# A graph network of three layers on one core: weights that have only a bias between them multiplied once, the node's own rows added behind W1, and the last round's kept sums added by VectorE

## The chip, the cores and the metric

One NeuronCore of a Trainium2 chip. The metric is the device time of one execution in microseconds (us). The kernel before takes 2256.65 us (median of 3 runs, 2256.49 to 2256.9).

## What is computed

12,500 nodes with 64 values each, 400,000 edges (`src`, `dst`), three layers. In every layer each node adds up the messages of its neighbours, adds its own row, and goes through a small network of two weights:

```python
h = relu(layernorm(x))
for l in range(3):
    mlp = lambda z: relu(z @ W1[l] + b1[l]) @ W2[l] + b2[l]
    agg = segment_sum(mlp(h[dst]), src, 12500)
    h = mlp(h + agg)
return x + h @ Wf + bf
```

Between the ReLU of one layer and the next ReLU stand only `@ W2[l] + b2[l]` and `@ W1[l+1] + b1[l+1]`, and behind the last ReLU `@ W2[2] + b2[2]` and `@ Wf + bf`.

## The kernel before

The sum over the edges is done as dense matmuls. A first part sorts nothing but counts: from windows of the edge list it builds a matrix of edge counts (12,544 by 12,544, two counts of 4 bits to a byte) in `counts_dram`. Then `agg` is messages times counts. The messages are held as two halves of 16 bits (`parts`, an upper half made by ScalarE and a lower half made by VectorE, both scaled by a power of two from the largest message, so that `scal[:, l, 6:7]` undoes the scale). A tile of counts is 128 by 896 columns and comes by DMA, 7 tiles (784 KB) to a transfer; VectorE unpacks it into low and high nibbles (`spread`).

The columns are cut into SB = 7 stretches of 4 banks of 448 columns. A bank is one PSUM bank and collects its sum over 98 tiles of 128 rows.

**Layer 0** runs while the counts are built. The rows come in 7 rounds of 14 tiles; a unit is one round for one stretch, so there are 49 units, numbered 0 to 48. 41 of them (FUSED) run inside the build, the other 8 behind it. Since PSUM can't hold 28 banks, each unit's sum is copied out (`keep_sums`, ScalarE, into `acc_low`, which lies in `msg`, and `acc_high`), and the next round's unit begins by adding it again with a matmul by the identity (`add_kept`, L1331). Units 42 to 48 are the last round, one for each stretch, and their sums are read by VectorE.

**Layers 1 and 2** have 7 stretches each, of CH = 14 chunks; a chunk is 7 tiles for 4 banks, 28 matmuls of 448 columns (L1438). The first and the last chunk of a stretch go bank by bank.

Behind each stretch comes its epilogue, spread over the next stretch's chunks (or, in layer 0, over the next unit's blocks, by the table MLP_AT). In the kernel before:

- `read_sums` (VectorE, L881 and L882): for each bank two instructions of 64 partitions each, one that only scales the sum, one that scales it and adds the node's own rows from `hT`; into `zP`.
- u0, u1 (TensorE, L1392): `W1` times `zP`, in PSUM banks 4 and 5; ScalarE adds b1 and applies ReLU into `U` (L1200).
- h (TensorE, L1400): `W2` times `U`; ScalarE adds b2 into `hN` (L1209), and GpSimd copies it to `hT` as the own rows of the next layer (`save_h`, L619).
- v (TensorE, L1400 too): the next layer's `W1` times `hN`; ScalarE adds its b1, ReLU, into `V` (L1213).
- m0, m1 (TensorE, L1416): `V` times the next `W2`, which gives the next messages; VectorE adds b2 and finds the largest (`finish`, L894 and L897). In the last layer there is no v, and m multiplies `hN` by `Wf` and VectorE adds bf and x (L904, L909).

All matmuls of the epilogue are of 32-bit numbers, and each stands in the trace as two matmul records.

Engines work through their instructions in program order, so the place of a step in an engine's list decides what waits behind it. Three places matter here. In the last round VectorE does, for unit i, `read_sums` of unit i-1, `unpack_tail` of its second chunk, `finish` of unit i-2, `unpack_tail` of the next unit's first chunk. Between layer 0 and layer 1 it does `find_peak` (L811), unpacks one chunk, then `make_scale` (L821 to L825), which waits for GpSimd's maximum over the partitions (`share_peak`, L613), then four `lower_parts` (L832), then `read_sums` of unit 48, for which TensorE's first chunk of layer 1 waits. And behind the first stretch of layer 1 it runs `judge` (L805, L806), two long reductions that check the counts.

The build is 49 steps of HG = 4 groups (k = 0 to 195): VectorE makes one-hot tiles (L752), GpSimd weighs them (L627), TensorE multiplies them (L1307), ScalarE keeps the product (`keep_batch`, L1132), VectorE transposes it (L760). In groups 0 to 25 ScalarE also makes layer 0's first rows (L1092), `keep_h0` (L1122) and the ReLU of W1 times them (L1183).

## Time and profile before

| | |
|---|---|
| median of 3 runs | 2256.65 us |
| the profiled execution | 2256.61 us, of which the span of the trace is 2254.9 us |
| TensorE busy (PE, matmuls) | 2096.7 us, 93% |
| VectorE busy (DVE) | 1512.7 us, 67% |
| ScalarE busy (ACT) | 663.7 us, 29% |
| GpSimd busy (POOL) | 643.7 us, 29% |
| mean granted TensorE clock | 0.976 of full speed |
| DMA engines | 153 GB/s on average |

The profile has one row for each group of instructions by line of the kernel, a chain of waits followed back from the last instruction, and a timeline. PE is TensorE's matmul part and PEld its weight loads, which overlap. The span falls into setup (to about 75 us), build with layer 0's units 0 to 40 (to about 950 us), the units 41 to 48 (to 1104 us), layer 1 (to 1675 us) and layer 2 (to the end).

### The profile page before, as it was taken

Reading aid. Unit: us, or ns where it says so; the run is one execution under the profiler, and the core shown is the slowest. Engines: PE = TensorE matmul, PEld = TensorE weight load, DVE = VectorE, ACT = ScalarE, POOL = GpSimd, SP = SyncE. Lnnn points to the kernel's source line nnn. Section 1 sums busy time; section 2 is a strip of 40 time slices with the busy share of each in tenths; the row PEclk is TensorE's granted clock in tenths of the full one; section 3 lists DMA queues with packets and bytes.
Section 4 is the critical chain, followed back from the end, with each engine's and each line's share of the span. In section 5 each row is a group of like instructions: output and inputs, shape, how many; then the busy total and the mean of one; then the engine's idle time right before and its main releaser. Section 6 shows DMA issues by size and latency. Waiting matters only on the chain.

```text
span 2254.9 us, 39446 instructions
## 1 busy us (share of the span) xinstructions
PE 2096.7 (93%) x15866; PEld 1153.6 (51%) x15866; DVE 1512.7 (67%) x1683; ACT 663.7 (29%) x1632; POOL 643.7 (29%) x287
## 2 busy tenths in 40 slices
PE   3566779999999999999997999999999999999998
PEld 3444445555555555545553555555555555555554
DVE  7899999999999999846645434444463443444344
ACT  4885655555555555411200000000010000000000
POOL 3666667777767776500000000000000000000000
PEclk8796999999999999999998999999999999999999
DMA  7256666666666666642343435444444554555552
GB/s 194 71 139 180 178 181 189 182 188 196 190 188 193 185 187 176 186 125 72 122 127 110 146 111 160 151 128 145 143 132 134 157 165 126 169 159 159 145 157 68
DMA packets 332824, 344.46 MB, mean 153 GB/s; under 512 B 21562, under 2 KB 303992, under 8 KB 332184
## 3 DMA queue, kind: packets, MB, share of 16 engines
q1 hardware_dynamic: 327516, 335.59, 50.6%
q0 software_dynamic: 2352, 6.43, 1.1%
q8 instruction: 94, 1.54, 0.3%
q10 hardware_dynamic: 2816, 0.53, 0.2%
q14 instruction: 46, 0.38, 0.0%
HBM read 252.58 MB, written 89.89 MB: 152 GB/s over the span
## 4 chain that ended last, share of the span: by engine, by line
PE 80%; DVE 13%; issue 4%; DMA 2%; SPq 0%; ACT 0%; POOL 0%; DVEq 0%; POOLq 0%
PE ps L1438 46%; PE ps L1336 18%; DVE arena L752 6%; PE ps L1331 5%; PE ps L1307 5%; PE ps L1400 2%; DVE arena L760 2%; PE ps L1392 2%; PE ps L1416 1%; DMA arena<-counts_dram 1%; DVE arena L791 1%; DVE arena L799 1%; DVE arena L725 1%; SPq L439 0%; DVE msg L778 0%
## 5 line engine op out<-in xcount | busy, mean ns | idle before, releaser
L1438 PE MATMUL ps<-arena,parts 128*128 128x448 fp8e4 x5488 | 1054.0, 353 | 11.9 <-DVE arena L882 11.9
L1438 PEld LDWEIGHTS ps<-arena,parts 128*128 128x128 f16 x5488 | 535.1, 98 | 531.4 <-issue 44.7
L627 POOL TENSOR_TENSOR arena<-arena,weight_now 128x416 int32<-128x416 int32 x196 | 540.8, 2759 | 274.0 <-DVE arena L752 273.3
L866 DVE TENSOR_SCALAR arena<-arena 128x3136 uint16<-128x3136 uint16 x196 | 191.5, 977 | 624.5 <-PE ps L1438 617.9
L1336 PE MATMUL ps<-arena,parts 128*128 128x448 fp8e4 x2744 | 554.9, 353 | 1.5 <-DVE parts L832 1.5
L752 DVE TENSOR_TENSOR arena<-row_iota,key_now 128x4096 f16<-128x4096 f16 x196 | 446.3, 2277 | 0.0
L1336 PEld LDWEIGHTS ps<-arena,parts 128*128 128x128 f16 x2744 | 267.1, 98 | 296.9 <-issue 83.1
L1132 ACT ACTIVATE arena<-ps 128x800 uint16<-128x800 f32 x392 | 332.3, 874 | 73.2 <-PE ps L1307 64.1
L1200 ACT ACTIVATE arena<-ps,b1s 128x448 f32<-128x448 f32 x42 | 26.6, 634 | 943.5 <-PE ps L1392 943.5
L1307 PE MATMUL ps<-arena 128*128 128x53 fp8e4 x6272 | 204.3, 189 | 79.8 <-DVE arena L752 41.2
L1307 PEld LDWEIGHTS ps<-arena 128*128 128x128 f16 x6272 | 187.7, 98 | 151.4 <-DVE arena L752 95.5
L619 POOL COPY hT<-arena 128x896 f32 (+1 forms) x14 | 13.2, 945 | 699.5 <-ACT arena L1209 699.5
L760 DVE STREAM_TRANSPOSE arena<-arena 128x800 int32<-128x800 int32 x196 | 195.2, 996 | 3.7 <-DMA counts_dram<-arena 3.7
L867 DVE TENSOR_SCALAR arena<-arena 128x3136 uint16<-128x3136 uint16 x196 | 190.0, 969 | 0.0
L647 POOL PARTITION_ALL_REDUCE good<-good x1 | 0.4, 409 | 526.8 <-DVE good L1000 526.8
L752 DVE TENSOR_TENSOR arena<-word_iota,key_now 128x832 uint16<-128x832 f16 x196 | 113.5, 579 | 4.6 <-ACT weight_now L1111 4.6
L1141 ACT ACTIVATE msg<-ps 128x448 f32<-128x448 f32 x84 | 45.7, 544 | 163.7 <-PE ps L1336 163.7
L1331 PE MATMUL ps<-msg,ident 128*128 128x448 f32 x168 | 83.2, 577 | 3.0 <-DVE arena L851 3.0
L1331 PE MATMUL ps<-arena,ident 128*128 128x448 f32 x168 | 83.1, 576 | 0.0
L1141 ACT ACTIVATE arena<-ps 128x448 f32<-128x448 f32 x84 | 45.7, 544 | 118.9 <-PE ps L1336 118.9
L607 POOL DMA_INDIRECT arena<-edges_dram,start_i x49 | 76.5, 1562 | 8.0 <-issue 3.5
L791 DVE TENSOR_SCALAR arena<-arena 128x3136 uint16<-128x3136 uint16 x82 | 76.2, 930 | 3.1 <-DMA arena<-counts_dram 3.0
(127 smaller groups left out, 1146.9 us busy)
## 6 DMA issues: line engine op xcount, KB each, us to landing
arena<-counts_dram SPq DMA_DIRECT2D x294, 784.0 KB, 4.6
counts_dram<-arena SPq DMA_DIRECT2D x784, 100.0 KB, 2.2
h_dram<-parts SPq DMA_DIRECT2D x2, 1536.0 KB, 7.2
edges_dram<-arena SPq DMA_DIRECT2D x2, 1400.0 KB
arena<-in_x_dram SPq DMA_DIRECT2D x14, 192.0 KB
out_dram<-arena SPq DMA_DIRECT2D x14, 192.0 KB
arena<-in_dst_dram SPq DMA_DIRECT2D x1, 1400.0 KB
arena<-in_src_dram SPq DMA_DIRECT2D x1, 1400.0 KB
```

The lines of the kernel that those rows point to most:

```text
L627: nc.gpsimd.tensor_tensor(pairs, pairs, weight_now[:, h * HW:(h + 1) * HW].unsqueeze(2).to_broadcast([P, HW, WORDS // 2]), ALU.mult).then_ ...
L752: return v.tensor_tensor(out, numbers.rearrange("p (m two) -> p m two", two=2).unsqueeze(1).to_broadcast(shape), key.unsqueeze(2).to_broad ...
L760: v.transpose(ctile[:, k % 2, :].bitcast(I32), stage[:, k % 2, :].bitcast(I32)).then_inc(s["counts_turned"], 1)
L791: v.tensor_scalar(spread[:, n % WIDE, 0, :].bitcast(U16), ring0[:, n % RING0, :].bitcast(U16), 0x0F0F, None, ALU.bitwise_and).then_inc(s[" ...
L866: v.tensor_scalar(spread[:, c % WIDE, 0, :].bitcast(U16), packed, 0x0F0F, None, ALU.bitwise_and)
L867: v.tensor_scalar(spread[:, c % WIDE, 1, :].bitcast(U16), packed, 4, 0x0F0F, ALU.logical_shift_right, ALU.bitwise_and).then_inc(s["counts_ ...
L1132: a.activation(to, product(q)[:, :, 0:2 * LP].rearrange("p c (m two) -> p c m two", two=2), ACT.Copy, scale=1.0 / WEIGHT_UNIT)
L1141: a.activation(kept_sums(u % SB, b), ps[:, bank, 0:NB], ACT.Copy).then_inc(s["sums_kept"], 1)
L1307: last = t.matmul(product(q)[:, c, 0:COLS], hot_r[:, slot, w, :], hot_c8[:, slot, w, 0:COLS], start=True, stop=True)
L1331: t.matmul(ps[:, bank, 0:NB], ident[:], kept_sums(u % SB, b), start=True, stop=False)
L1336: last = t.matmul(ps[:, bank, 0:NB], parts[:, (ROUND * (u // SB) + c) * CK + k, :], spread[:, c, b // 2, at:at + NB].bitcast(F8), start=u ...
L1438: last = t.matmul(ps[:, b, 0:NB], parts[:, c * CK + k, :], spread[:, c % WIDE, b // 2, at:at + NB].bitcast(F8), start=start, stop=stop)
```

## The change

1. In group 38 of the build (FUSE_AT) TensorE transposes the three `W2b`, in group 39 it multiplies each by the next `W1b` (the last by `Wfb`), and the biases between them as columns; ScalarE writes the products over `W1b[1]`, `W1b[2]`, `Wfb` and makes `b1_next`; VectorE makes `bf_last` in group 40.
2. `hT` now holds the own rows behind W1 and with their bias. ScalarE writes them, in the build (a new activation beside the ReLU of each block) and in the epilogue (L1200 of the list of before becomes a ReLU of VectorE's sum). GpSimd's `save_h` is gone.
3. The epilogue is u0, u1, own, m0, m1 (the last one u0, u1, m0, m1). `add_own` on VectorE adds u and the own rows into `U`.
4. `read_sums` is one instruction of 128 partitions for each bank, banks in the order 0, 2, 1, 3.
5. In the last round `add_kept` is gone; the kept sums are scaled when they are kept and added by VectorE in `read_sums`.

```diff
-MLP_AT = {1: (0,), 2: (1,), 3: (2,), 5: (3,), 7: (4, 5)}
+MLP_AT = {2: (0, 1), 4: (2,), 7: (4, 5)}
+pe.wait_ge(s["weights_fused"], 2)
...
# read_sums, VectorE
-for b in range(SBB):
-    dve.wait_ge(s["sums_done"], (UNITS - SB + g) * SBB + b + 1)
-    v.tensor_scalar(zP[other, cols], ps[other, b, 0:NB], scal[other, l, 6:7], None, ALU.mult)
-    v.scalar_tensor_tensor(zP[own, cols], ps[own, b, 0:NB], scal[own, l, 6:7],
-                           hT[own, ds(i * SBH + b % 2 * NB, NB)], ALU.mult, ALU.add)
+for n, b in enumerate(BANKS):
+    dve.wait_ge(s["sums_done"], (UNITS - SB + g) * SBB + n + 1)
+    if l == 0:
+        v.scalar_tensor_tensor(zP[:, cols], ps[:, b, 0:NB], scal[:, 0, 6:7], kept_sums(i, b), ALU.mult, ALU.add)
+    else:
+        v.tensor_scalar(zP[:, cols], ps[:, b, 0:NB], scal[:, l, 6:7], None, ALU.mult)
+def add_own(l, i, b):
+    dve.wait_ge(s["u_done"], g * 2 + b + 1)
+    v.tensor_tensor(U[:, b * NB:(b + 1) * NB], ps[:, 4 + b, 0:NB], hT[:, ds(i * SBH + b * NB, NB)], ALU.add)
...
# the last round, VectorE
 if i:
     read_sums(0, i - 1)
+    add_own(0, i - 1, 0)
+    add_own(0, i - 1, 1)
 unpack_tail(n + 1)
...
# a stretch, VectorE, for c in range(1, CH)
 unpack(i, l, c, 0)
+if c in (2, 3):
+    add_own(*before, c - 2)
...
# epilogue, ScalarE
+a.activation(U[:, cols], U[:, cols], ACT.Relu)
 for b in range(2 if l < L - 1 else 0):
+    a.activation(hT[:, ds(i * SBH + b * NB, NB)], ps[:, 4 + b, 0:NB], ACT.Identity, bias=b1_next[:, l:l + 1])
     a.activation(V[:, b * NB:(b + 1) * NB], ps[:, 4 + b, 0:NB], ACT.Relu,
-                 bias=b1s[:, l + 1:l + 2])
+                 bias=b1_next[:, l:l + 1])
...
# the build, ScalarE, blocks 0 to 12
+a.activation(hT[:, m * MB * P:m * MB * P + n], ps[:, 0, 0:n], ACT.Identity, bias=b1s[:, 0:1])
 a.activation(uS[:, 0:n], ps[:, 0, 0:n], ACT.Relu, bias=b1s[:, 0:1])
...
# TensorE, stages of the epilogue
-steps = ["u0", "u1", "h", "v", "m0", "m1"] if not final else ["u0", "u1", "h", "", "m0", "m1"]
+steps = ["u0", "u1", "own", "", "m0", "m1"] if not final else ["u0", "u1", "", "", "m0", "m1"]
```

What this moves on the engines, at the three places that the prediction speaks of. First TensorE in one unit of the last round, before (L1336 are the blocks of 7 count matmuls, L1331 the kept sums, L1392 u, L1400 h and v, L1416 m):

```order
L1331 MATMUL ps<-msg,ident 128x448
L1336 MATMUL ps<-arena,parts 128x448 x7
L1392 MATMUL ps<-arena,W1s 64x448 x2
L1331 MATMUL ps<-msg,ident 128x448
L1336 MATMUL ps<-arena,parts 128x448 x7
L1392 MATMUL ps<-arena,W1s 64x448 x2
L1331 MATMUL ps<-arena,ident 128x448
L1336 MATMUL ps<-arena,parts 128x448 x7
L1400 MATMUL ps<-arena,W2b 128x448 x2
L1331 MATMUL ps<-arena,ident 128x448
L1336 MATMUL ps<-arena,parts 128x448 x14
L1400 MATMUL ps<-arena,W1b 128x448 x2
```

and with the change (L1363 are the blocks, L1440 u, L1446 own, L1462 m):

```order
L1363 MATMUL ps<-arena,parts 128x448 x21
L1440 MATMUL ps<-arena,W1s 64x448 x4
L1363 MATMUL ps<-arena,parts 128x448 x14
L1446 MATMUL ps<-arena,W1b 128x448 x2
L1363 MATMUL ps<-arena,parts 128x448 x21
L1462 MATMUL ps<-W2b,arena 128x128 x7
```

The four kept sums and one of the two stages of L1400 are gone, and both u stand together behind the unit's second block.

Second, VectorE in a unit of the last round, with the change (L874 reads a bank's sum, L888 adds the own rows, L845 and L846 unpack a chunk, L899 and L902 are `finish`):

```order
L874 SCALAR_TENSOR_TENSOR arena<-ps,scal,msg 128x448
L874 SCALAR_TENSOR_TENSOR arena<-ps,scal,arena 128x448
L888 TENSOR_TENSOR arena<-ps,hT 128x448 x2
L845 TENSOR_SCALAR arena<-arena 128x3136
L846 TENSOR_SCALAR arena<-arena 128x3136
L899 TENSOR_TENSOR msg<-ps,b2row 128x512
L902 TENSOR_REDUCE peak<-msg 128x1
```

Before, eight instructions of 64 partitions stood where now four of L874 stand (two are shown), and the unpacking followed them at once; now the two additions, which wait for u, come ahead of it.

Third, ScalarE in an odd group of the early build, with the change (L1147 and L1149 keep the counts, L1213 is the ReLU, L1124 and L1126 keep the keys of the next step):

```order
L1147 ACTIVATE arena<-ps 128x16x25x2
L1149 ACTIVATE row_edges<-ps 128x16
L1212 ACTIVATE hT<-ps,b1s 128x512
L1213 ACTIVATE uS<-ps,b1s 128x512
L1124 COPY key_now<-ps 128x256
L1126 CAST weight_now<-ps 128x64
```

L1212 is new, 13 times in all, ahead of the ReLU and of the keys.

## Rows read from the trace of the kernel before

**Rows 1.** The page, part 1: busy time of each engine.
```profile
PE 2096.7 (93%) x15866; PEld 1153.6 (51%) x15866; DVE 1512.7 (67%) x1683; ACT 663.7 (29%) x1632; POOL 643.7 (29%) x287
```

**Rows 2.** The page, part 4: shares of the chain that ended last.
```profile
PE 80%; DVE 13%; issue 4%; DMA 2%; SPq 0%; ACT 0%; POOL 0%; DVEq 0%; POOLq 0%
```

**Rows 3.** Groups by line and shape, from 900 us on: busy us, mean ns.
```profile
L1331 PE MATMUL ps<-arena,ident 128*128 128x448 f32 x44 | 21.3, 565 | 0.0
L1400 PE MATMUL ps<-arena,W2b 128*128 128x448 f32 x84 | 35.2, 541 | 0.0
L1400 PE MATMUL ps<-arena,W1b 128*128 128x448 f32 x56 | 23.3, 539 | 0.0
```

**Rows 4.** Chain in order of time: start, us; from one unit of the last round.
```profile
1021.76 1.32 PE ps L1336 x7
1023.09 0.75 PE ps L1331 x2
...
1025.16 0.90 PE ps L1392 x4
1026.07 0.95 PE ps L1331 x2
...
1040.57 1.56 PE ps L1416 x14
1042.13 1.32 PE ps L1336 x7
```

**Rows 5.** The same view, second stretch of layer 1: stage h and the chunk behind it.
```profile
1211.40 0.90 PE ps L1392 x4
1212.31 5.40 PE ps L1438 x28
1217.71 1.50 PE ps L1400 x4
1219.21 5.30 PE ps L1438 x28
```

**Rows 6.** Groups by line and shape from 900 us on, VectorE.
```profile
L881 DVE TENSOR_SCALAR arena<-ps,scal 64x448 f32<-64x448 f32 x84 | 57.2, 682 | 17.9 <-PE ps L1336 11.6 <-PE ps L1438 4.4 <-DVE good L807 0.3
L832 DVE SCALAR_TENSOR_TENSOR parts<-msg,scal,parts 128x448 f16<-128x448 f32 x28 | 17.8, 678 | 2.7 <-ACT parts L1161 2.7
L894 DVE TENSOR_TENSOR msg<-ps,b2row 128x512 f32<-128x512 f32 x9 | 6.2, 690 | 0.2
```

**Rows 7.** Timeline of the step from layer 0 to layer 1, GpSimd, VectorE.
```profile
1090.33 0.38 POOL L613 PARTITION_ALL_REDUCE scal<-scal  x1 [14.81 <-DVE scal L811]
...
1096.30 0.98 DVE L866 TENSOR_SCALAR arena<-arena 128x3136 uint16<-128x3136 uint16 x1 [6.11 <-PE ps L1336]
...
1098.08 0.15 DVE L821 TENSOR_SCALAR scal<-scal 128x1 f32<-128x1 f32 x1
1100.35 2.47 DVE L832 SCALAR_TENSOR_TENSOR parts<-msg,scal,parts 128x448 f16<-128x448 f32 x4 [1.36 <-ACT parts L1161]
```

**Rows 8.** Windows: length, busy of PE, PEld, DVE, ACT, POOL, PEclk, DMA, GB/s.
```profile
953.40:957.00 3.60, 3.53 (x9) 1.56 (x10) 1.78 (x3) 0.00 (x0) 0.00 (x0) 0.59 0.29 63
1196.00:1200.00 4.00, 2.74 (x8) 1.19 (x9) 3.89 (x7) 0.00 (x0) 0.00 (x0) 0.50 0.00 0
```

**Rows 9.** Timeline, TensorE, the waits behind the build and behind `judge`.
```profile
953.47 1.86 PE L1331 MATMUL ps<-msg,ident 128*128 128x448 f32 x2 [2.99 <-DVE arena L851]
1197.26 7.84 PE L1438 MATMUL ps<-arena,parts 128*128 128x448 fp8e4 x28 [11.90 <-DVE arena L882]
```

**Rows 10.** Windows of the early build, and ScalarE's ReLU and the row behind it.
```profile
120.00:140.00 20.00, 11.94 (x182) 9.79 (x181) 19.93 (x19) 18.40 (x51) 14.38 (x6) 0.91 0.58 148
140.00:160.00 20.00, 12.14 (x193) 9.39 (x188) 19.90 (x20) 17.74 (x48) 13.04 (x6) 0.91 0.46 110
126.04 0.73 ACT L1183 ACTIVATE uS<-ps,b1s 128x512 f32<-128x512 f32 x1
126.61 0.43 ACT L1109 COPY key_now<-ps 128x256 f16<-128x256 f16 x1
```

**Rows 11.** Timeline, the end of the program.
```profile
2231.68 8.68 PE L1438 MATMUL ps<-arena,parts 128*128 128x448 fp8e4 x45
...
2241.59 0.63 ACT L1200 ACTIVATE arena<-ps,b1s 128x448 f32<-128x448 f32 x1 [60.38 <-PE ps L1392]
...
2245.43 1.83 PE L1416 MATMUL ps<-Wfb,arena 128*128 128x128 f32 x14 [0.72 <-ACT arena L1209]
```

More of the change, by code:

```diff
@@ L1140, in keep_sums, with copy_weights, keep_weights @@
                     act.wait_ge(s["parts_made"], ROUND * (u + 1))
-                a.activation(kept_sums(u % SB, b), ps[:, bank, 0:NB], ACT.Copy).then_inc(s["sums_kept"], 1)
+                a.activation(kept_sums(u % SB, b), ps[:, bank, 0:NB], ACT.Copy,
+                             scale=scal[:, 0, 6:7] if u >= UNITS - 2 * SB else 1.0).then_inc(s["sums_kept"], 1)
+            def copy_weights():
+                act.wait_ge(s["weights_turned"], 1)
+                a.copy(uS[:, 0:3 * P], ps[:, 2, 0:3 * P])
+                a.activation(uS[0:D, 3 * P:4 * P], ones[0:D, :], ACT.Copy, scale=b2s[0:D, L - 1:L]).then_inc(
+                    s["weights_copied"], 1)
+            def keep_weights():
+                act.wait_ge(s["weights_multiplied"], 1)
+                for l in range(L - 1):
+                    a.copy(W1b[:, l + 1, :], ps[:, 2, l * P:(l + 1) * P])
+                    a.activation(b1_next[:, l:l + 1], ps[:, 2, 3 * P + l:3 * P + l + 1], ACT.Identity, bias=b1s[:, l + 1:l + 2])
+                a.copy(Wfb[:], ps[:, 2, (L - 1) * P:L * P]).then_inc(s["weights_fused"], 1)
             def upper_parts(l, n):
@@ L1336, in multiply_chunk @@
                     last = t.matmul(ps[:, bank, 0:NB], parts[:, (ROUND * (u // SB) + c) * CK + k, :],
[L1337 removed]
+                                    spread[:, c, b // 2, at:at + NB].bitcast(F8), start=(u < SB or u >= UNITS - SB) and c == 0 and k == 0,
                                     stop=stop and k == CK - 1)
@@ L1354, in add_bank, with turn_weights, multiply_weights @@
                 last.then_inc(s["sums_done"], 1)
+            def turn_weights():
+                pe.wait_ge(s["scale_made"], 1)
+                for l in range(L):
+                    last = t.transpose(ps[:, 2, l * P:(l + 1) * P], W2b[:, l, :], ident[:])
+                last.then_inc(s["weights_turned"], 1)
+            def multiply_weights():
+                pe.wait_ge(s["weights_copied"], 1)
+                for l in range(L):
+                    later = W1b[:, l + 1, :] if l < L - 1 else Wfb[:]
+                    t.matmul(ps[:, 2, l * P:(l + 1) * P], uS[:, l * P:(l + 1) * P], later, start=True, stop=True)
+                    if l < L - 1:
+                        t.matmul(ps[:, 2, 3 * P + l:3 * P + l + 1], later, b2s[:, l:l + 1], start=True, stop=True)
+                t.matmul(ps[:, 2, 3 * P + L:3 * P + L + D], uS[0:D, 3 * P:4 * P], Wfs[:], start=True, stop=True).then_inc(
+                    s["weights_multiplied"], 1)
             for k in range(BUILD * HG):
                 j, h = k // HG, k % HG
+                if k == FUSE_AT:
+                    turn_weights()
+                if k == FUSE_AT + 1:
+                    multiply_weights()
                 if k == SCALE_AT:
@@ L1430, in multiply_stretch @@
                     if c in (0, CH - 1):
-                        steps.sort(key=lambda step: step[1])
+                        steps.sort(key=lambda step: BANKS.index(step[1]))
                     for k, b in steps:
@@ L1444, in multiply_stretch @@
                     mlp_stage(*before, c)
-            MLP_AT = {1: (0,), 2: (1,), 3: (2,), 5: (3,), 7: (4, 5)}
+            MLP_AT = {2: (0, 1), 4: (2,), 7: (4, 5)}
+            pe.wait_ge(s["weights_fused"], 2)
             for u in range(FUSED, UNITS):
                 i = u - (UNITS - SB)
+                banks = range(SBB) if i < 0 else BANKS
                 for c in range(ROUND):
```

105 lines of the change are left out of this document (53 added, 52 removed).

## The prediction

> **What bounds the kernel now.** I read the shares of busy time first: TensorE is busy for 93% of the span, VectorE for 67% [rows 1]. An average says little, so I went to the chain that ended last: 80% of it is TensorE [rows 2]. In order of time this chain holds nothing but TensorE's matmuls from the units behind the build to the end, except at three places: a wait of 2.99 us where unit 41 begins, one of 11.90 us behind `judge` [rows 9], and the ending. In the chain a stage of the epilogue stands in line with the count matmuls: the chunk comes when the stage's 1.50 us are over [rows 5]. So behind the build every microsecond that leaves TensorE's list leaves the time, as long as nothing else then arrives late. Up to about 340 us VectorE sets the pace (19.93 of 20 us [rows 10]), and the change takes nothing from it there.
>
> **What the change takes from TensorE.** A matmul of 448 columns of 32-bit numbers stands as two records, of 565 ns in the groups [rows 3]; these are modelled and overlap, so the chain's steps count: 0.75 us for one kept sum (two records), 0.90 us for a u, 1.50 us for a stage of two banks, 1.56 us for m [rows 4, 5].
>
> - Last round, kept sums: 7 units of 4, 28 x 0.75 = 21.0 us. In six units two of the four stand right behind a u and take 0.95 [rows 4], 12 x 0.20 = 2.4 more; whatever stands behind a u keeps some of it (the chunk behind one takes 5.40, another 5.30 [rows 5]), and the two u now stand together, so 6 x 0.10 = 0.6 comes back. Gain 22.8 us.
> - Stages h and v become one, `own`, of the same form as each (128 x 128 weights, 448 columns): 7 stretches in layer 0 and 7 in layer 1, 14 x 1.50 = 21.0 us.
> - In layer 2 stage h goes and nothing takes its place: 6 x 1.50 = 9.0 us. The seventh is in the ending.
> - Behind `judge` TensorE waits for the first bank's reading. That was two instructions of VectorE, 0.68 us each [rows 6], and is one: 0.7 us. `judge` itself stays, and so do the rest of the 11.90 us and the slow matmuls behind it [rows 8, 9].
> - Ending: the last block ends at 2240.36 (2231.68 + 8.68) and m begins at 2245.43 [rows 11], 5.07 us later. Now: two u (1.80), 0.1 to VectorE, one addition (0.65, between the 448 and 512 columns of [rows 6]), ReLU 0.63 [rows 11], 0.1 back: 3.3 us. Gain 1.8 us.
>
> Sum of the gains: 22.8 + 21.0 + 9.0 + 0.7 + 1.8 = 55.3 us.
>
> **Does anything arrive late in the shorter units?** A unit of the last round took 1042.13 - 1021.76 = 20.37 us [rows 4]; it will take 8 blocks x 1.32 + 1.80 + 1.50 + 1.56 = 15.4 us. VectorE's own work in it: four readings at 0.70 (128 partitions cost what 64 do: 678 ns for 128 x 448, 682 for 64 x 448 [rows 6]), two additions at 0.65, two chunks unpacked at 1.8, `finish` 2.5: 10.2 us. From the unit's start: both u are done at 4.45; the additions end at 5.2, the unpacking at 7.1, and TensorE wants that chunk at 8.6. ReLU ends at 6.0, and `own` is due at 7.1. Both are in time by 1.1 to 1.5 us. In the stretches the second addition stands behind the unpacking of chunk 3 and can begin 1.8 us after chunk 1 ends; with ReLU `own`'s input is there at 3.3, and TensorE comes to it at 6.2 (a u and chunk 2). The reading order 0, 2, 1, 3 is followed by TensorE's blocks, so u0 has its two banks first. GpSimd's copies were hidden and cost or give nothing; ScalarE has as many activations in an epilogue as before and is idle around them. The transfers (784 KB each) have to come every 5.3 us in the stretches as before, and in the last round every 7.7 us instead of every 10.2.
>
> **What the change adds.**
>
> - *The step from layer 0 to layer 1.* Count from the start of unit 48: TensorE is through at 15.4. VectorE: additions to 5.2, unpacking to 7.1, `finish` to 9.7, `find_peak` to 9.9, a chunk unpacked to 11.8, `make_scale` 0.9 to 12.7, ScalarE's first upper half 0.6 to 13.4, four lower halves 2.5 [rows 7] to 15.9, the first reading to 16.7. TensorE waits 1.3 us where it didn't wait before, provided that GpSimd's maximum is there within 1.6 us of its start. Before, it began at 1090.33 and VectorE used it at 1098.08 without a wait of its own [rows 7]; so it takes between the 0.38 us of its row and 7.75 us. The row is of a GpSimd instruction whose record is rough. I take 2.8 us, what GpSimd's largest elementwise instruction takes in the early build (L627, the page), since this one has less data but must cross the partitions. That is 1.2 us over, so the wait is 2.5 us; ends 1.3 and 7.5.
> - *The clock behind that wait.* After 2.99 us of waiting [rows 9] the granted clock was 0.59 in the next 3.6 us, after 11.90 us it was 0.50 [rows 8], the lower of the two levels (1.2 against 2.4 GHz). The latter cost 7.84 - 5.30 = 2.5 us on one chunk [rows 5, 9]. A wait of 2.5 us may or may not do this: half, 1.3 us; ends 0 and 2.6.
> - *ScalarE in the early build.* 13 activations more; one takes 0.57 us until the next begins (126.61 - 126.04) [rows 10]. ScalarE was busy for 18.40 and 17.74 of 20 us there; a block comes about every 8.7 us, so it gets 1.3 us more in 20, and has 1.6 to 2.3 free. It fits, barely: I take 0.4 us; ends 0 and 7.4 (13 x 0.57, nothing hidden).
> - *The fused weights.* TensorE waits for ScalarE's copy in group 39, ScalarE for TensorE, VectorE in group 40 for ScalarE; VectorE is the bound there and gets one addition, 0.15 us, and a wait that its lead over the other engines may or may not allow. I take 0.6 us in all; ends 0.1 and 3.
>
> Losses: 2.5 + 1.3 + 0.4 + 0.6 = 4.8 us. Net 55.3 - 4.8 = 50.5 us. Against the profiled execution's own 2256.61 us (span 2254.9, and 1.7 around it, which stay) this gives 2206.1 us; that execution lies 0.04 under the median, which changes nothing.
>
> **The page that speaks against it.** The trace shows GpSimd's maximum with a row of 0.38 us and a bound of 7.75 [rows 7]. The Trainium skill, GPSIMD Engine Reference, section Instruction dispatch, says that the first call of a freshly loaded GpSimd routine pays a code load of about 6 us that no row of the profile shows. By that rule, with its figure as an estimate, the maximum would come 6 us after its start, and the time would be near 2211 us; no row here shows it, and the trace's bound allows it. Of the clock, the waits of 2.99 and 11.90 us were followed by the lower level [rows 8, 9]; TensorE: Matmul & The Clock Gate, section HAM oscillation, says that an idle gap between bursts returns the array to that level, and by this rule the trace agrees.
>
> **Rivals.**
>
> 1. *The maximum is slow.* Its cost shows nowhere before because 7.75 us were free. If it takes all of them, the wait is 7.5 us and the clock falls for certain: 55.3 - 7.5 - 2.6 - 1.0 = 44.2, time 2212.4 us. For it: the rough record. Against: its row.
> 2. *ScalarE becomes the bound of the early build.* 7.4 us instead of 0.4: 2213.1 us. For it: 18.40 of 20 us. Against: VectorE takes a group's counts only two groups later, so ScalarE may lag a little.
> 3. *TensorE's list is shorter but its place is taken by waiting in the last round*: if VectorE's additions came later than reckoned by over 1.5 us, chunk 1 of each unit would wait and give back what is saved there. All of the 6 x 4.9 us lost: about 2235 us. Against: the 1.1 to 1.5 us of room, and VectorE's 10.2 of 15.4 us.
> 4. *It doesn't reach the end*: if transfers set the pace of the stretches, the saved 30 us there would become waits for counts, and with rival 3 the time would be within 0.2% of before. Against: in the build more is moved in the same time (about 186 GB/s against 140 in the stretches, the page's GB/s line), and no wait for counts stands in the chain.
> 5. *Slower: the wait of rival 3 with the clock behind it.* VectorE's unpacking of a unit's second chunk now stands behind its two additions, and these wait for u. If TensorE then waited about 3 us for that chunk in each unit, as it did once at unit 41, the clock could fall each time as it did there [rows 8, 9]. A unit holds 15.4 us of matmuls, and at the lower level they take 15.4 more. Slower than before begins where the six units lose 55 us, 9.2 each: 3 of waiting and 6.2 from 40% of the unit's matmuls at the lower level. With all of them at it: 6 x 18.4 = 110 us, 2316 us. It decides once the additions end 4.5 us later than reckoned, against 10.2 us of work in 15.4: very unlikely.
>
> **How the numbers follow.** My case with its bounds (2202.5 to 2209.5) gets 0.66; rival 1, the page's 6 us with it, 0.18; rival 2 0.08; rival 3 in part or whole 0.04; rival 4 0.015; rival 5 0.01; the rest for gains beyond my sum. Without any of the four losses but the 1.3 us, the time is 2202.6 us. The range reaches from 2201.5 to 2213, which leaves out rival 2 in its full size with rival 1, and rivals 3 to 5. Under 0.2% (4.5 us) this kernel's measurement can't tell a change from none; faster by more has 0.97, within it 0.015, slower 0.015.
>
> **What would show it.** A unit of the last round at 15.4 us in the chain and no kept sums behind unit 41; a stretch shorter by 1.5 us; stage `own` at 1.50 us, with no wait for ReLU; a new wait at the first chunk of layer 1, its length telling the maximum's cost, and the clock behind it; the time at which the build ends (946 to 950 us before) later by under 1.5 us. If the build ends 3 us later or more, ScalarE or the fused weights are to blame. If chunks of the stretches wait for counts, or `own` for ScalarE, the forecast's ground is gone.

## The result and the profile after

The changed kernel takes 2203.5 us (median of 4 runs, 2202.36 to 2206.4) against 2256.78 us (2256.49 to 2258.93) for the kernel before on the same chip: ratio 0.9768, 95% interval 0.9754 to 0.9783, so 53.3 us less. The profiled execution took 2206.40 us with a span of 2204.6 us, 50.2 us under the profiled execution of before. The forecast was 2206.1 us, in a range of 2201.5 to 2213.

The page, part 1, and the shares of the chain in part 4, which answer to [rows 1, 2]:

```profile
PE 2046.7 (93%) x15741; PEld 1131.8 (51%) x15741; DVE 1474.5 (67%) x1642; ACT 658.9 (30%) x1638; POOL 631.5 (29%) x273
...
PE 72%; DVE 18%; issue 5%; DMA 2%; ACT 1%; SPq 1%; POOL 0%; DVEq 0%; POOLq 0%; ACTq 0%
```

TensorE's busy time fell by 50.0 us and the span by 50.3. The share is 93% both times: the bound didn't move to another engine. The chain's share of TensorE, 80% before and 72% here, says nothing of the change: a second trace of the kernel before has 72%, one of the change 56%. What differs between them is how much of the build the chain follows through VectorE.

One unit of the last round, from the chain in order of time (start, us, engine, line, matmuls). It answers to [rows 4]:

```profile
1015.22 3.97 PE ps L1363 x21
1019.20 1.65 PE ps L1440 x8
1020.85 2.75 PE ps L1363 x14
1023.60 1.50 PE ps L1446 x4
1025.11 3.97 PE ps L1363 x21
1029.08 1.56 PE ps L1462 x14
1030.64 3.97 PE ps L1363 x21
```

From one 3.97 to the next the same way, 1030.64 - 1015.22 = 15.42 us, where it was 20.37. All is matmuls, and no wait stands between them. The two u together take 1.65, where two separate ones took 1.80 [rows 4]; this is worth 6 x 0.15 = 0.9 us and stands in no term of the forecast's sum.

The same view, second stretch of layer 1, as in [rows 5]:

```profile
1176.24 0.90 PE ps L1440 x4
1177.14 5.40 PE ps L1484 x28
...
1188.85 1.50 PE ps L1446 x4
```

`own` costs what h and v cost each, and a chunk behind a u takes the 5.40 that it took: none waits for its counts.

The groups by line and shape from 900 us on, VectorE, as in [rows 6] (busy us, mean ns; then idle time and what ended it):

```profile
L877 DVE TENSOR_SCALAR arena<-ps,scal 128x448 f32<-128x448 f32 x56 | 37.8, 681 | 23.7 <-PE ps L1484 23.3 <-DVE good L802 0.3
L888 DVE TENSOR_TENSOR arena<-ps,hT 128x448 f32<-128x448 f32 x42 | 26.0, 620 | 19.0 <-PE ps L1440 18.2
```

A reading of 128 partitions takes 681 ns where one of 64 took 682 [rows 6]; the new addition takes 620.

The four waits of TensorE that are left behind the build (us in total, times, longest):

```profile
PE ps L1484 <- DVE arena L877: 11.1, 1, 11.1
PE ps L1358 <- DVE arena L846: 4.8, 1, 4.8
PE ps L1462 <- ACT arena L1235: 1.4, 1, 1.4
PE ps L1484 <- DVE arena L874: 0.7, 1, 0.7
```

They are the wait behind `judge`, the one for the first unpacked counts behind the build (unit 41), the ending, and the only new one, at the first chunk of layer 1. There is none of L1446 (`own`) for ScalarE and none of L1363 for VectorE's unpacking, on which rivals 3 and 5 rested.

The new wait, from the timeline of the step from layer 0 to layer 1 (start, us, engine, instruction, in brackets the idle time before it). It answers to [rows 7]:

```profile
1061.31 4.14 PE L1363 MATMUL ps<-arena,parts 128*128 128x448 fp8e4 x21
...
1066.47 1.38 DVE L888 TENSOR_TENSOR arena<-ps,hT 128x448 f32<-128x448 f32 x2 [2.95 <-PE ps L1440]
...
1067.88 0.58 ACT L1235 ACTIVATE arena<-arena 128x448 f32<-128x448 f32 x1 [0.17 <-DVE arena L888]
...
1069.69 1.67 PE L1446 MATMUL ps<-arena,W1b 128*128 128x448 f32 x4
...
1072.32 1.68 POOL L620 PARTITION_ALL_REDUCE scal<-scal  x1 [123.00 <-DVE scal L806]
1072.99 0.97 DVE L862 TENSOR_SCALAR arena<-arena 128x3136 uint16<-128x3136 uint16 x1
1074.03 0.15 DVE L816 TENSOR_SCALAR scal<-scal 128x1 f32<-128x1 f32 x1
...
1075.75 2.47 DVE L827 SCALAR_TENSOR_TENSOR parts<-msg,scal,parts 128x448 f16<-128x448 f32 x4 [0.81 <-ACT parts L1190]
...
1078.14 0.68 DVE L874 SCALAR_TENSOR_TENSOR arena<-ps,scal,msg 128x448 f32<-128x448 f32 x1
...
1078.96 5.46 PE L1484 MATMUL ps<-arena,parts 128*128 128x448 fp8e4 x28 [0.74 <-DVE arena L874]
```

The first row is the last block of unit 47 and the first two of unit 48, 1.32 us each, so unit 48 begins at 1062.63. The additions end 5.2 us later (1067.85), ReLU 5.8 (1068.46), and `own` starts at 7.1. GpSimd's maximum takes 1.68 us this time and is done at 1074.00, just as VectorE is through with the chunk that it unpacks meanwhile (1073.96). TensorE then waits 0.74 us.

Windows (length; busy of PE, PEld, DVE, ACT, POOL; granted clock, DMA share, GB/s), as in [rows 8]: unit 41, the first chunk of layer 1, the chunk behind `judge`.

```profile
958.60:962.20 3.60, 3.52 (x8) 1.43 (x9) 1.75 (x2) 0.00 (x0) 0.00 (x0) 0.50 0.43 95
1078.90:1084.00 5.10, 5.04 (x27) 2.67 (x28) 5.07 (x8) 1.78 (x4) 0.00 (x0) 1.00 0.48 128
1169.40:1176.00 6.60, 6.51 (x28) 3.02 (x28) 3.49 (x5) 0.00 (x0) 0.00 (x0) 0.79 0.26 66
```

Behind 4.78 us of waiting the clock was at the lower level (0.50), behind 0.74 us it stayed at the upper one. Behind `judge` it rose within the chunk, and the timeline, which answers to [rows 9], has that chunk at 6.75 us instead of 7.84. Both places differ from one execution of a kernel to the next, as the second trace will show.

```profile
958.68 1.83 PE L1358 MATMUL ps<-msg,ident 128*128 128x448 f32 x2 [4.78 <-DVE arena L846]
1169.49 6.75 PE L1484 MATMUL ps<-arena,parts 128*128 128x448 fp8e4 x28 [11.14 <-DVE arena L877]
```

The windows of the early build, for [rows 10], and the timeline of the ending, for [rows 11]:

```profile
120.00:140.00 20.00, 13.21 (x196) 10.43 (x195) 19.02 (x20) 18.87 (x52) 12.13 (x6) 0.81 0.53 130
140.00:160.00 20.00, 11.43 (x164) 8.91 (x164) 19.83 (x19) 18.74 (x48) 14.14 (x6) 0.91 0.42 99
```

```profile
2183.66 8.30 PE L1484 MATMUL ps<-arena,parts 128*128 128x448 fp8e4 x43
...
2194.48 0.58 ACT L1235 ACTIVATE arena<-arena 128x448 f32<-128x448 f32 x1 [0.27 <-DVE arena L888]
2195.11 1.83 PE L1462 MATMUL ps<-Wfb,arena 128*128 128x128 f32 x14 [1.40 <-ACT arena L1235]
```

ScalarE has 18.87 and 18.74 of 20 us where it had 18.40 and 17.74. The last block ends at 2191.96 and m begins 3.15 us later, against 5.07 before.

**Where the time went.** It helps to cut the span where unit 41 begins: behind it TensorE never stops but for the waits above. In the trace of before, 2254.9 - 953.47 = 1301.4 us lie behind the cut, in that of the change 2204.6 - 958.68 = 1245.9: 55.5 us less. In the same traces the build ends 5.2 us later. The experiments ask whether the first number is made of the terms that the forecast gave it, and whether the second is a cost of the change.

### The profile page after: what moved, and what is told of

Its sections match the earlier page's. It is cut to its first block, busy times and chain, and to the rows that moved or that the text cites. A ratio compares the mean times of both kernels' runs of the same rounds, so it can differ in the third digit from the quotient of the medians.

```text
span 2204.6 us, 39047 instructions
## 1 busy us (share of the span) xinstructions
PE 2046.7 (93%) x15741; PEld 1131.8 (51%) x15741; DVE 1474.5 (67%) x1642; ACT 658.9 (30%) x1638; POOL 631.5 (29%) x273
## 4 chain that ended last, share of the span: by engine, by line
PE 72%; DVE 18%; issue 5%; DMA 2%; ACT 1%; SPq 1%; POOL 0%; DVEq 0%; POOLq 0%; ACTq 0%
PE ps L1484 47%; PE ps L1363 13%; DVE arena L747 9%; PE ps L1334 4%; DVE arena L755 3%; PE ps L1358 3%; PE ps L1440 2%; DMA arena<-counts_dram 2%; PE ps L1462 1%; PE ps L1446 1%; DVE arena L786 1%; DMA counts_dram<-arena 1%; DVE arena L794 1%; SPq L446 1%; DVE arena L720 1%
## 5 line engine op out<-in xcount | busy, mean ns | idle before, releaser
L861 DVE TENSOR_SCALAR arena<-arena 128x3136 uint16<-128x3136 uint16 x196 | 191.3, 976 | 606.6 <-PE ps L1484 606.6
L1363 PE MATMUL ps<-arena,parts 128*128 128x448 fp8e4 x2744 | 553.9, 354 | 1.9 <-DVE parts L827 1.9
L1363 PEld LDWEIGHTS ps<-arena,parts 128*128 128x128 f16 x2744 | 267.4, 98 | 294.4 <-issue 77.5
L1147 ACT ACTIVATE arena<-ps 128x800 uint16<-128x800 f32 x392 | 333.7, 881 | 65.0 <-PE ps L1334 57.8
L1235 ACT ACTIVATE arena<-arena 128x448 f32<-128x448 f32 x42 | 24.2, 577 | 1001.5 <-DVE arena L888 1001.5
L862 DVE TENSOR_SCALAR arena<-arena 128x3136 uint16<-128x3136 uint16 x196 | 190.1, 970 | 0.0
L786 DVE TENSOR_SCALAR arena<-arena 128x3136 uint16<-128x3136 uint16 x82 | 77.0, 939 | 6.8 <-DMA arena<-counts_dram 6.7
L614 POOL DMA_INDIRECT arena<-edges_dram,start_i x49 | 76.3, 1557 | 8.0 <-issue 4.7
L794 DVE TENSOR_SCALAR arena<-arena 128x3136 uint16<-128x3136 uint16 x82 | 76.6, 934 | 0.0
L1156 ACT ACTIVATE msg<-ps 128x448 f32<-128x448 f32 x70 | 38.1, 545 | 127.7 <-PE ps L1363 125.8
L1149 ACT ACTIVATE row_edges<-ps 128x16 f16<-128x16 f32 x392 | 75.5, 193 | 0.0
L1358 PE MATMUL ps<-msg,ident 128*128 128x448 f32 x140 | 70.2, 584 | 4.8 <-DVE arena L846 4.8
```

The source lines that it names most:

```text
L786: v.tensor_scalar(spread[:, n % WIDE, 0, :].bitcast(U16), ring0[:, n % RING0, :].bitcast(U16), 0x0F0F, None, ALU.bitwise_and).then_inc(s[" ...
L794: v.tensor_scalar(spread[:, n % WIDE, 1, :].bitcast(U16), ring0[:, n % RING0, :].bitcast(U16), 4, 0x0F0F, ALU.logical_shift_right, ALU.bit ...
L861: v.tensor_scalar(spread[:, c % WIDE, 0, :].bitcast(U16), packed, 0x0F0F, None, ALU.bitwise_and)
L862: v.tensor_scalar(spread[:, c % WIDE, 1, :].bitcast(U16), packed, 4, 0x0F0F, ALU.logical_shift_right, ALU.bitwise_and).then_inc(s["counts_ ...
L1147: a.activation(to, product(q)[:, :, 0:2 * LP].rearrange("p c (m two) -> p c m two", two=2), ACT.Copy, scale=1.0 / WEIGHT_UNIT)
L1358: t.matmul(ps[:, bank, 0:NB], ident[:], kept_sums(u % SB, b), start=True, stop=False)
```

## The experiments

"Behind the cut" is the span less the start of unit 41. The first four ran on one chip, the next four on a second, the three with a moved arena on a third, the last on a fourth; each beside the kernel before on the same chip. Between chips the ratios compare, the microseconds only roughly.

**The change again.** Expected:

> The changed kernel itself, beside the others on the same chip. It ran at 2203.5 us (2202.36 to 2206.4). Both theories expect that again, 52 to 54 us under before, and in its trace 15.4 us for a unit of the last round. The theory of TensorE's list says that the gain is the matmuls taken from TensorE; the rival says that much of it comes from VectorE, whose eight half readings for a stretch became four whole ones. A third question is the end of the build, which lay 5.2 us later than before in the profiled run (958.68 against 953.47 us): if that was the change's own, it comes again; if it was one execution's transfers, it comes out under 3 us here.

Measured: 2204.63 us (2200.64 to 2206.81), ratio 0.9756 (0.9743 to 0.9768), 1245.9 us behind the cut, unit 41 at 959.14: the late end of the build came again. That the part behind the cut repeats to 0.1 us is luck. From unit 41 to the first u it is 987.60 - 959.14 = 28.46 us here and 988.29 - 958.68 = 29.61 in the first trace, and the chunk behind `judge` takes 7.86 here and took 6.75 there. The first trace's u, then the second's, and the second's chunk and window of unit 41:

```profile
988.29 1.72 PE L1440 MATMUL ps<-arena,W1s 128*64 128x448 f32 x8
```

```profile
987.60 1.72 PE L1440 MATMUL ps<-arena,W1s 128*64 128x448 f32 x8
...
1168.81 7.86 PE L1484 MATMUL ps<-arena,parts 128*128 128x448 fp8e4 x28 [11.14 <-DVE arena L877]
```

```profile
959.10:962.70 3.60, 3.56 (x9) 1.60 (x10) 1.71 (x2) 0.00 (x0) 0.00 (x0) 0.59 0.44 93
```

So two differences of 1.1 us, both of the clock behind a wait, cancelled. This second trace is the better one to set against the first trace of before, since both have 0.59 at unit 41 [rows 8] and nearly the same chunk behind `judge` (7.86 and 7.84): 1301.43 - 1245.86 = 55.57 us. The next experiments are compared with it, and the two places are taken out where they matter.

**The kept sums back on TensorE**, and kept unscaled.

```diff
 # TensorE, last round
+if i >= 0:
+    add_kept(u, b, b)
...
 # read_sums, l == 0, VectorE
-v.scalar_tensor_tensor(zP[:, cols], ps[:, b, 0:NB], scal[:, 0, 6:7], kept_sums(i, b), ALU.mult, ALU.add)
+v.tensor_scalar(zP[:, cols], ps[:, b, 0:NB], scal[:, 0, 6:7], None, ALU.mult)
...
 # keep_sums, ScalarE
-             scale=scal[:, 0, 6:7] if u >= UNITS - 2 * SB else 1.0).then_inc(s["sums_kept"], 1)
+             scale=1.0).then_inc(s["sums_kept"], 1)
...
```

> One part undone: in the last round the kept sums go back to TensorE, 28 matmuls by the identity, and VectorE only scales; all else as in the change. TensorE's list: 28 x 0.75 = 21.0 us more, at most 1 us of it given back at the step to layer 1, where the wait of 0.74 us goes; so 20 to 22 us over the changed kernel. The rival: VectorE's readings keep their number and length, so nearly all of the gain stays, under 5 us over the changed kernel.

Measured: 2224.45 us (2222.57 to 2228.04), ratio 0.9846 (0.9834 to 0.9859), 19.8 us over the change; 1266.3 us behind the cut, 20.4 more. The chain of its third unit:

```profile
1013.78 1.50 PE ps L1444 x4
...
1022.14 0.75 PE ps L1356 x2
...
1027.95 0.95 PE ps L1356 x2
...
1032.30 1.50 PE ps L1444 x4
```

A unit lasts 18.52 us instead of 15.42: three kept sums at 0.75 and the one behind u at 0.95, less the 0.1 that the block behind the two u no longer keeps. That is 6 x 3.1 and 3.0 in the first unit, 21.6 us, less 0.7 because the wait at layer 1's first chunk is gone: 20.9 against the 20.4 measured, of which 0.1 is the chunk behind `judge` (7.72 us here). VectorE's half of the trade costs nothing that shows.

**Stage `own` twice** (the same matmuls once more into the same bank, so the result is the same).

```diff
 # TensorE, stage own, for each bank
+t.matmul(ps[:, 4 + b, 0:NB], W1b[:, l + 1, :], U[:, b * NB:(b + 1) * NB], start=True, stop=True)
 t.matmul(ps[:, 4 + b, 0:NB], W1b[:, l + 1, :], U[:, b * NB:(b + 1) * NB], start=True, stop=True)
```

> Stage own multiplies each bank twice (the second result overwrites the first, which is the same), so 14 stages cost two more matmuls of 448 columns each, as h and v did. TensorE's list: 14 x 1.50 = 21.0 us over the changed kernel. The rival, or a cost that hides beside waits: under 5 us.

Measured: 2222.36 us (median of five, 2220.9 to 2224.34; a sixth run at 3101.03 is left out), ratio 0.9841 (0.9828 to 0.9853), 17.7 us over the change; 1266.5 us behind the cut, 20.6 more, of 21.0 reckoned, with layer 1's first wait (0.7) gone here too and the chunk behind `judge` at 8.22. Each of the 14 stages costs its 1.50 us. The times differ by less than 20.6 because the build ended early here (unit 41 at 952.69 in the trace, against 959.14).

**The readings in halves of 64 partitions again** (layer 0's, which add the kept sums, in the same way).

```diff
 # read_sums, l > 0, VectorE
-v.tensor_scalar(zP[:, cols], ps[:, b, 0:NB], scal[:, l, 6:7], None, ALU.mult).then_inc(
-    s["sums_read"], 1)
+for r in (slice(0, D), slice(D, P)):
+    last = v.tensor_scalar(zP[r, cols], ps[r, b, 0:NB], scal[r, l, 6:7], None, ALU.mult)
...
+last.then_inc(s["sums_read"], 1)
```

> Each reading of a bank by VectorE is two instructions of 64 partitions again, as before the change; TensorE's list is untouched. TensorE's list: only the three places where TensorE waits for a reading pay, 0.6 to 0.7 us each (behind judge, at the step from layer 0 to layer 1, and 0.6 at the end), so 1 to 2.5 us over the changed kernel. The rival: a large part of the 53 us comes back, over 15 us.

Measured: 2206.39 us (2204.3 to 2208.35), ratio 0.9764 (0.9751 to 0.9776), 1.8 us over the change, within the two intervals. The trace tells more (waits of TensorE behind the build):

```profile
PE ps L1486 <- DVE arena L879: 11.8, 1, 11.8
PE ps L1486 <- DVE arena L875: 1.4, 1, 1.4
...
PE ps L1442 <- DVE arena L879: 0.8, 1, 0.8
```

Each of the three places where TensorE waits for a reading is 0.7 to 0.8 us longer, 2.2 us together; 4.0 more lie behind the cut, and 1.5 of them are slower matmuls in unit 41 (29.99 us to the first u instead of 28.46; granted clock 0.68 from 960.2 to 964 us, where the change's second trace has 1.00 from 962.7 to 966). In all other places the second halves (84 in all) are hidden. Halving VectorE's instructions was worth its three waits and no more.

**A useless stage in layer 2**, in the place of the old h.

```diff
-steps = ["u0", "u1", "own", "", "m0", "m1"] if not final else ["u0", "u1", "", "", "m0", "m1"]
+steps = ["u0", "u1", "own", "", "m0", "m1"] if not final else ["u0", "u1", "extra", "", "m0", "m1"]
...
+elif kind == "e":
+    for b in range(2):
+        wait_alone(pe, s["u_kept"], g * 2 + b + 1)
+        t.matmul(ps[:, 4 + b, 0:NB], W2b[:, l, :], U[:, b * NB:(b + 1) * NB], start=True, stop=True)
```

> Layer 2 gets a stage of two matmuls back, as h was, but nothing waits for its result. TensorE's list: 6 x 1.50 = 9.0 us in the stretches, and up to 1.5 us at the end, where m may now wait behind it; 9 to 10.5 us over the changed kernel. If the end isn't set by TensorE in layer 2 but by the counts, under 3 us.

Measured: 2214.83 us (2211.0 to 2218.28), ratio 0.9811 (0.9796 to 0.9826); 1256.1 us behind the cut, 10.2 more than the change's 1245.9. Of these, 1.4 are a slower unit 41 (29.87 us to the first u), and the chunk behind `judge` gives 1.0 back (6.88 us); the stages cost 9.8. At the ending m begins 4.01 us behind the last block instead of 3.15, 0.9 more, since the extra stage fills part of a wait; the six others make 9.0. The saved 9.0 us of layer 2 were real: no transfer or unpacking would have filled their place.

**Without layer 0's own rows in the build.** The 13 new activations of ScalarE are left out, so `hT` keeps the rows ahead of W1 and this kernel's output is another.

```diff
 # the build, ScalarE, blocks 0 to 12
-a.activation(hT[:, m * MB * P:m * MB * P + n], ps[:, 0, 0:n], ACT.Identity, bias=b1s[:, 0:1])
```

> Leaves out layer 0's own rows behind W1: the 13 activations of ScalarE in the early build (hT keeps the rows ahead of W1, so the output is another). If ScalarE is near its limit there, 13 x 0.57 = 7.4 us come off the changed kernel; by my forecast 0.4 us, and from the traces at most 1.4 us, which these runs can hardly tell from none. In the trace VectorE's group 28 comes 0 to 1.4 us earlier after its group 10 (76.0 us apart before, 75.9 to 77.4 us in the change's traces).

Measured: 2202.87 us (2201.26 to 2203.71), ratio 0.9758 (0.9745 to 0.9771), the change's own ratio. VectorE's transpose of group 26 starts at 184.6 here, 112.4 us behind the first; in the ten other traces with these activations 111.8 to 113.2 (112.5 on average), in the three of the kernel before 111.9 to 112.7. From its group 10 to its group 28, of which the expectation spoke, it is 76.3 us, inside the 75.9 to 77.4 of the traces with the activations. So no cost of the activations shows above a scatter of 1.3 us, and the 7.4 us of rival 2 are out, though ScalarE falls from 18.87 and 18.74 to these:

```profile
120.00:140.00 20.00, 12.37 (x199) 10.31 (x198) 19.72 (x21) 18.23 (x52) 12.84 (x6) 0.90 0.55 137
140.00:160.00 20.00, 11.43 (x164) 8.80 (x164) 19.93 (x19) 16.88 (x45) 14.24 (x6) 0.91 0.43 102
```

**The kernel before again.**

> The kernel before, for a second trace of it. In its first trace VectorE ended the build at 950.66 us and waited 3.0 us for transfers of counts; in five traces with the change's build it ended at 949.8 to 956.3 us, with 3.2 to 7.0 us of such waits. If the change made the build longer, this trace ends it near 951 us again and the change's stay above; if it is one execution's transfers, this one may end anywhere from 950 to 956 us.

Measured: 2256.24 us (2253.58 to 2258.77), ratio 0.9993 (0.9984 to 1.0002); 1302.1 us behind the cut, unit 41 at 952.04. VectorE's last transpose of the build starts at 949.24, against 950.66 in the first trace of this kernel and 949.8 to 956.3 in the eight traces of kernels with the change as it stands; the early end came again, but the two ranges touch. Behind the cut unit 41 is slower here and the chunk behind `judge` faster (6.95 us for 7.84): what looked like a gain of the change at `judge` comes without it too.

**`judge` in pieces.** The longest wait left was 11.14 us behind `judge`, with slower matmuls behind it. Its two reductions of 6272 numbers become eight of 1568, spread over chunks 4 to 7 and 10 to 13 of the last stretch, where VectorE idles up to 3.9 us ahead of a chunk.

```diff
+def judge_piece(n):
+    half, q = n % 2, n // 2
+    rows = slice(q * BUILD * QN // 4, (q + 1) * BUILD * QN // 4)
+    last = v.tensor_reduce(judged[:, half, q:q + 1], row_edges[:, rows, :], AX.XY, (ALU.add, ALU.max)[half])
+    if n == 7:
+        link(last, dve)
+        judge()
...
+if last and l == L - 1 and c in JUDGE_AT:
+    judge_piece(JUDGE_AT.index(c))
...
-if l == 1:
-    judge()
```

> The changed kernel, with judge taken out of the step from the first to the second stretch of layer 1 and cut into eight reductions of a quarter of its data each (1.65 us, by 6.60 us for the whole), one behind each of eight chunks of the last stretch, where VectorE has about 3.4 us free per chunk. TensorE's list: the wait of 11.1 us goes, and with it the chunk at a lower clock (6.75 instead of 5.30 us), so 12 to 13 us under the changed kernel, near 2191 us, and no new wait in the last stretch. If another wait stands behind the first (counts that come late because the loads are held up), less than 6 us.

Measured: 2189.99 us (2187.19 to 2192.27), ratio 0.9700 (0.9686 to 0.9714), 14.6 us under the change on the other chip; by the ratios, 0.9756 against 0.9700, 12.6. 1233.4 us behind the cut, 12.4 less. One piece in VectorE's timeline:

```profile
2115.83 0.98 DVE L871 TENSOR_SCALAR arena<-arena 128x3136 uint16<-128x3136 uint16 x1 [3.91 <-PE ps L1494]
...
2117.61 1.78 DVE L809 TENSOR_REDUCE judged<-row_edges 128x1 f32<-128x1568 f16 x1
2121.12 0.98 DVE L871 TENSOR_SCALAR arena<-arena 128x3136 uint16<-128x3136 uint16 x1 [1.74 <-PE ps L1494]
```

The 3.91 us of idle time shrink to 1.74 and nobody waits. 11.14 of waiting and 7.86 - 5.30 = 2.56 of slower matmuls are 13.7 us; unit 41 was 1.2 us slower in this trace (29.70 to the first u), which leaves 12.5, against the 12.4 measured. This version beats both kernels.

**The arena's address.** The two new on-chip tensors, 268 bytes on each partition, are declared ahead of the big arena and move its address. To learn whether this makes the build end later, the kernel before got the two tensors, unused, and the change got them behind the arena, with and without `judge` in pieces.

```diff
 # the kernel before
+b1_next = sb("b1_next", [P, L], F32)
+bf_last = sb("bf_last", [P, D], F32)
 arena = sb("arena", [P, ARENA], U8)
 # the change
-b1_next = sb("b1_next", [P, L], F32)
-bf_last = sb("bf_last", [P, D], F32)
 arena = sb("arena", [P, ARENA], U8)
+b1_next = sb("b1_next", [P, L], F32)
+bf_last = sb("bf_last", [P, D], F32)
```

> The kernel before with the two new on-chip tensors (the fused bias and the row for the last plies' weights, 268 bytes on each partition) declared ahead of the big arena and never used, so that the arena's address moves as the change moves it, and nothing else changes. Theory A, the address makes the build's transfers and transposes slower: unit 41 starts about 3 us later than in the kernel before (at about 956 against 952 to 953.5), and the run is about 3 us over the kernel before (ratio 1.0013). Rival, the later end of the build comes from the change's own instructions or from chance: unit 41 starts at 952 to 953.5 and the ratio is within 0.9990 to 1.0005.

> The change with the two new tensors declared behind the arena, so that the arena has the address that it had before. Theory A: unit 41 starts at 952 to 954, and the run takes about 2201 us, 3 us less than the change. Rival, the change's own instructions or chance: unit 41 starts between 955 and 959 as in most of the other traces with the change, and the run is within 1.5 us of 2204. The span behind the start of unit 41 is 1246 us by either.

> The change with the judged rows' reduction in pieces (which took 14.6 us off the change) and the two new tensors behind the arena. Theory A: 3 us less than with the pieces alone, about 2187 us. Rival: 2190 us, within 1.5. The span behind the start of unit 41 is 1233 to 1234 us by either.

Measured: the kernel before with the moved arena 2258.13 us (2254.57 to 2261.2), ratio 0.9999 (0.999 to 1.0007), unit 41 at 955.76. The change with the arena in its old place 2201.12 us (2200.62 to 2202.34), ratio 0.9743 (0.973 to 0.9755), unit 41 at 954.33. With `judge` in pieces 2188.98 us (2185.77 to 2190.34), ratio 0.9689 (0.9676 to 0.9701), unit 41 at 953.24. The first two starts went theory A's way or nearly so. Of the times only the second did: the first ratio is not the 1.0013 of theory A, and 2188.98 us lies within the rival's 1.5 us of 2190. Behind the cut the last one has 1230.7 us where 1233 to 1234 were expected by either theory. Beside the second one (1244.5), which has the same 27.01 us from unit 41 to the first u, this is 13.8 us for `judge`; the second one waits 11.14 us there and takes 7.91 for the chunk behind, and 11.14 + (7.91 - 5.30) are 13.75. The second one was run once more.

> The same kernel as the change with its two new tensors behind the arena, run again on its own. Theory A, the arena's address costs about 3 us: unit 41 starts by 955 and the ratio is again near 0.9743, at any rate under 0.9750. Rival, the first run of it was low by chance: the ratio is like that of the change (0.9756 and 0.9768), and unit 41 starts anywhere between 952 and 959.

Measured: 2201.69 us (2199.65 to 2202.62), ratio 0.9756 (0.9742 to 0.9769), which is the change's own ratio; unit 41 at 954.06. In the time, the rival wins: no effect of the address is shown. In the traces a hint is left. In the five with the arena in its old place unit 41 starts at 952.04 to 954.33, in the nine with it moved at 952.69 to 959.14. The averages are 953.4 and 956.1. Fourteen single executions on several chips don't settle 2 or 3 us, and this stays open. The change declares the two tensors ahead of the arena, so if the address counts, it is a cost of the change as it stands.

## Why the prediction came out right

**Kept sums, 22.8 us.** Right. The undone part gave back 20.4 us; its own rows make 21.6, of which 0.7 hide in layer 1's first wait. With the new order of the two u it has only one kept sum behind a u in each unit; the second is worth 6 x 0.20 = 1.2, and 21.6 + 1.2 = 22.8.

**h and v to `own`, 21.0, and layer 2, 9.0.** Right: 20.6 us for the doubled stage; in layer 2 9.8 us, of which 0.9 at the ending. The unit came out at 15.42 of 15.4 forecast. But the sum took 4.8 us from each of six units, and 20.37 - 15.42 is 4.95: the two u that now stand together take 1.65 instead of 1.80, 0.9 us in all that no term held.

**`judge`, 0.7, and the ending, 1.8.** 11.90 - 11.14 = 0.76 and 5.07 - 3.15 = 1.92. The term supposed that the slow matmuls stay, and they do on no fixed terms: in the trace of the result the chunk took 1.09 us less than before, but over the nine traces of the change and its variants that have it, it takes 6.75 to 8.22, and in the three of the kernel before 7.84, 6.95 and 6.86. The granted clock over its first 6.6 us was 0.79 in that trace and 0.63 in the change's second one and in the first of before: the clock rises earlier or later in the chunk, with the change and without it.

**VectorE's additions in time (rivals 3 and 5).** From the start of unit 48 the additions ended at 5.2 (forecast 5.2), ReLU at 5.8 (6.0), unpacking at 7.0 (7.1), and `own` started at 7.1 (7.1). Both rivals fall, and so does rival 4: the stages added to layer 2's stretches cost their full length. (Rival 4's "saved 30 us there" was miscounted: six of the 14 stages h and v stand in the last round, so 21 us were saved in the stretches.)

**The step from layer 0 to layer 1, 2.5 us.** Too much: 0.74. The first reading ended at 16.2 us from the unit's start and not at 16.7, and TensorE was through at 15.6 and not at 15.4, so 0.6 us of waiting stand for the 1.3, and 0.1 for the signal. The other 1.2 us were GpSimd's maximum, taken at 2.8 us from an elementwise instruction. It took 1.68, VectorE's chunk beside it took as long, and so it cost nothing. This is the mis-sized term: the 2.8 us. The wait as a whole was forecast 1.76 us too long, 1.2 of it by the maximum.

The Trainium skill, GPSIMD Engine Reference, section Instruction dispatch, has a first call of a freshly loaded routine pay about 6 us that no row shows. The trace shows no such time: VectorE used the first maximum 1.71 us after it began. The second took 0.35. Whether the routine was freshly loaded at that point no row tells. Rival 1 falls by the 1.71.

**The clock behind that wait, 1.3 us.** Nothing: behind 0.74 us of waiting the granted clock was 1.00.

**ScalarE in the early build, 0.4 us.** Not contradicted: leaving the activations out moved nothing above a scatter of 1.3 us. Rival 2 falls: at 18.8 of 20 us ScalarE still isn't the bound.

**The fused weights, 0.6 us.** The four groups 36 to 40 took 19.1 and 19.2 us in the traces of before and 19.2 or 19.3 with the change: 0.1 us, the low end.

**The sum as measured, and the luck in it.** Behind the cut the gains are 22.8 + 21.0 + 9.0 + 0.76 + 1.92 and the 0.9 of the joined u, 56.4, less 0.74 for the new wait: 55.6 us, against the 55.6 measured between the two traces that are alike at unit 41 and behind `judge`. The forecast had 51.5 there (55.3 less 2.5 and 1.3). The 4.1 between them are the wait at the step to layer 1 (1.76), the clock (1.3), the joined u (0.9) and small parts of the two terms above (0.2). The sum nevertheless fitted the profiled execution to 0.3 us, because that execution's build ended 5.2 us later, where 1.0 was reckoned. Two errors of about 4 us each cancelled in it, and that is luck. By the medians the change gains 53.3 us, 2.8 more than forecast, and 54.1 in the second measurement, so 1.5 to 2.3 us are lost ahead of the cut; 0.1 of it is shown to come from the weights, none is shown to come from the activations, and the rest is open.

The sign given at the end of the prediction, that the build ends less than 1.5 us later, and 3 us only if ScalarE or the fused weights are to blame, was wrong: their costs are 0.1 us and nothing that shows, and the kernel before with a moved arena also ended its build 2.3 to 3.7 us later than in its two other traces. The end of the build scatters by more than the effect looked for.

## What to carry to other kernels

Where one engine stands in the chain without a gap, count what leaves its list by the chain's own steps, not by the modelled length of its records: 14 stages of 1.50 us, the extra ones of layer 2 and 28 kept sums all came out within a few per cent. Count also what new neighbours cost: two stages of one form side by side took 1.65 us, apart 1.80. Where another engine gets the work, reckon its finishing times from the start of one unit; then the room (here over 1 us) says whether the trade is free. After such a change look at the waits that remain: a check of 13 us that could have been in pieces from the start was worth a quarter of the whole change. And cut the span where one engine hardly idles behind it: the part behind the cut was 1244.5 to 1246.5 us in the five traces that differ only ahead of it, while the build ended anywhere within 6 us. Even then look inside before you trust an agreement or explain a difference of 1 us: behind each wait of several us the clock can come back earlier or later, and twice 1245.9 was two such differences that cancelled.
